# Bias products and turned row maxima on the full array, with zero rows, in a four-layer attention and expert kernel

## The reference

```
x += L0_xattn(layernorm(x), ctx)    # 16 heads of 8; biases on q, k, v and on the output
x += L0_ffn(layernorm(x))           # 8 experts, top 1, 128 -> 512 -> 128, gelu, biases b1, b2
x += L1_xattn(layernorm(x), ctx)    # 16 heads of 64, output bias
x += L1_ffn(layernorm(x))           # 128 -> 512 -> 128, rounded, piecewise linear gelu, biases
x += L2_xattn(layernorm(x), ctx)    # layernorm; self attention (causal) + ffn; layernorm; cross attention + ffn
x += L2_ffn(layernorm(x))           # 8 experts, top 2, silu, biases
x += L3_xattn(layernorm(x), ctx)    # 16 heads of 8, no bias
x += L3_ffn(layernorm(x))           # 8 experts, top 1, no bias on the output
```

## Time and profile before

| what | value |
|---|---|
| three runs | 1269.59, 1274.54 and 1707.18 us, median 1274.54 |
| span of the profiled execution | 1272.0 us |
| PE busy | 978.4 us (77%), 15468 products |
| DVE busy | 832.6 us (65%) |
| ACT busy | 735.7 us (58%) |
| POOL busy | 550.4 us (43%) |
| chain that ended last | PE 43%, DVE 25%, ACT 13%, issue 9%, POOL 5%, DMA 3% |
| mean granted TensorE clock | 0.870 of full speed |

### The profile page before, as it was taken

How to read it: one execution, slowest core, us unless ns; L and a number is a source line. 1 busy time by engine, 2 the same in 40 slices (tenths; PEclk the granted TensorE clock), 3 DMA queues, 4 the chain that set the end, 5 groups by cost and what they waited for, 6 DMA issues and landing times.

```text
span 1272.0 us, 38517 instructions
## 1 busy us (share of the span) xinstructions
PE 978.4 (77%) x15468; PEld 717.5 (56%) x15468; DVE 832.6 (65%) x2267; ACT 735.7 (58%) x1500; POOL 550.4 (43%) x575
## 2 busy tenths in 40 slices
PE   2778767989999867588998589988399956875874
PEld 1455556736767734345675256766287834654863
DVE  4667645688888588678877577767454647675532
ACT  5776454676665575576657467576265575763321
POOL 2565724345446344354361322221632475566132
PEclk9788678989999977799999699999599977786787
DMA  3321132211001010110001000000331121110122
GB/s 103 92 82 43 59 85 72 66 37 34 27 19 36 2 40 19 38 39 12 3 4 43 1 3 4 5 3 2 93 95 44 50 73 45 34 43 29 46 78 75
DMA packets 59727, 53.29 MB, mean 42 GB/s; under 512 B 10592, under 2 KB 47968, under 8 KB 59362
## 3 DMA queue, kind: packets, MB, share of 16 engines
q1 hardware_dynamic: 53777, 41.62, 11.4%
q0 software_dynamic: 4096, 8.40, 2.3%
q10 hardware_dynamic: 1683, 0.81, 0.2%
HBM read 33.90 MB, written 16.25 MB: 39 GB/s over the span
## 4 chain that ended last, share of the span: by engine, by line
PE 43%; DVE 25%; ACT 13%; issue 9%; POOL 5%; DMA 3%; POOLq 1%; ACTq 0%; SPq 0%; DVEq 0%
PE psum L698 16%; PE psum L1246 6%; PE psum L1264 5%; DVE area L1949 4%; POOL sorted_in L2882 3%; PE psum L821 2%; DVE stats L1930 2%; DVE negm L2085 2%; ACT area L1333 2%; ACT xn L1357 1%; PE psum L705 1%; DVE area L2117 1%; DVE x L2481 1%; PE psum L894 1%; PE psum L1223 1%
## 5 line engine op out<-in xcount | busy, mean ns | idle before, releaser
L1333 ACT ACTIVATE area<-psum 128x512 bf16<-128x512 f32 (+4 forms) x214 | 107.1, 525 | 126.0 <-PE psum L698 64.6
L1949 DVE TENSOR_TENSOR area<-psum,area 128x512 bf16<-128x512 f32 (+4 forms) x206 | 117.2, 601 | 44.3 <-ACT area L1333 43.2
L2592 DVE TENSOR_TENSOR area<-area 128x512 bf16<-128x512 f32 x106 | 73.1, 691 | 97.1 <-ACT area L1847 68.7
L1246 PE MATMUL psum<-xT_hi,moe 128*128 128x128 bf16 x848 | 111.0, 230 | 9.0 <-DVE xT_lo L1949 4.9
L2692 POOL TENSOR_TENSOR moe<-stage,moe 128x512 bf16<-128x512 f32 x47 | 54.8, 1168 | 123.2 <-ACT moe L1328 123.0
L1515 ACT ACTIVATE area<-psum 77x1024 f32<-77x1024 f32 (+1 forms) x96 | 92.8, 1017 | 23.8 <-PE psum L821 23.8
L1264 PE MATMUL psum<-moe,area 128*128 x1272 | 104.9, 224 | 0.9 <-DVE area L2601 0.9
L2085 DVE TENSOR_REDUCE negm<-psum 128x4 bf16<-128x308 f32 (+1 forms) x192 | 95.5, 540 | 12.4 <-PE psum L791 12.2
L1246 PEld LDWEIGHTS psum<-xT_hi,moe 128*128 x848 | 82.2, 103 | 20.8 <-issue 10.9
L1246 PE MATMUL psum<-xT_lo,moe 128*128 128x128 bf16 x424 | 93.7, 230 | 0.0
L1264 PEld LDWEIGHTS psum<-moe,area 128*128 128x128 bf16 x1272 | 85.3, 100 | 11.8 <-issue 1.4
(11 more groups left out here) (262 smaller groups left out, 2935.8 us busy)
## 6 DMA issues: line engine op xcount, KB each, us to landing
area<-sorted_in SPq DMA_DIRECT2D x22, 256.0 KB, 3.5
sorted_out<-area SPq DMA_DIRECT2D x22, 256.0 KB, 2.3
stage<-in_w_L0m SPq DMA_DIRECT2D x16, 256.0 KB, 2.9
stage<-in_w_L2m SPq DMA_DIRECT2D x16, 256.0 KB, 2.8
stage<-in_w_L3m SPq DMA_DIRECT2D x16, 256.0 KB, 2.7
sorted_in<-area SPq DMA_DIRECT2D x2, 1472.0 KB, 7.3
stage<-in_w_L2a SPq DMA_DIRECT2D x8, 320.0 KB, 3.3
stage<-in_w_L1x SPq DMA_DIRECT2D x6, 320.0 KB, 3.1
```

Of the source, the lines that this page charges most:

```text
L1246: ins = pe.matmul(bank[:, S * c:S * c + S], lhsT, v, start=n == 0, stop=n == 2)
L1333: ins = act.activation(out, bank, ACT.Copy)
L1949: ins = dve.tensor_tensor(out, bank, high, ALU.subtract)
L2592: dve.tensor_tensor(R.HL[u], R.HF[u], upper(R.HF[u]), ALU.subtract).then_inc(K.tile_split, tiles.one())
```

## The change

The tiles `pairs`, `pairs_L0b2`, `pairs_L2be2` and `ones` get 128 rows. POOL sets the three pair tiles to zero at the start, and DVE then writes the bias into rows 0 and 1 as before, so that a bias product uses 128 rows, 126 of them zero times one. In L1x the maxima go to a block of 128 x 128 (`A.NM`, two of them, in a tile that L1x does not use), which POOL sets to zero at the start of L1x; quarter `k` gets only its own four heads, at columns 36k to 36k+3, and one product turns the whole block. L2a1 and L2a2 keep the four products of 32 columns.

```diff
-        self.pairs = sb("pairs", [2, N_SHARED_PAIRS], BF16)
-        self.expert_pairs = {name: sb("pairs_" + name, [2, E * D], BF16) for name in ("L0b2", "L2be2")}
+        self.pairs = sb("pairs", [128, N_SHARED_PAIRS], BF16)
+        self.expert_pairs = {name: sb("pairs_" + name, [128, E * D], BF16) for name in ("L0b2", "L2be2")}
...
-        self.ones = sb("ones", [2, BANK], BF16)
+        self.ones = sb("ones", [128, BANK], BF16)
...
+        self.NM = [K.yT_hi[:, s, 0:128] for s in range(2)]
...
-            for r in range(4):
-                ins = pe.matmul(bank[32 * r:32 * r + 32, 0:S], K.negm[:, b % 2, :], K.ident_bf[:, :], start=True, stop=True)
+            if A.upright:
+                for r in range(4):
+                    ins = pe.matmul(bank[32 * r:32 * r + 32, 0:S], K.negm[:, b % 2, :], K.ident_bf[:, :], start=True,
+                                    stop=True)
+            else:
+                ins = pe.matmul(bank[:, 0:S], A.NM[b % 2], K.ident_bf[:, :], start=True, stop=True)
             filled(ins, name, "negm", b)
...
         sem.wait_ge(K.pair_copied, 1)
+        sem.wait_ge(K.pairs_zeroed, 1)
         for out, (at, n) in [(K.pairs, (0, N_SHARED_PAIRS))] + [(v, PAIRS[name]) for name, v in K.expert_pairs.items()]:
-            dve.scalar_tensor_tensor(out[:, :], K.pair_hi[:, at:at + n], K.col("pmask")[0:2, :],
+            dve.scalar_tensor_tensor(out[0:2, :], K.pair_hi[:, at:at + n], K.col("pmask")[0:2, :],
                                      K.pairs_raw[:, at:at + n], ALU.mult, ALU.add)
...
-                empty(dve.tensor_reduce(K.negm[:, s, 4 * k:4 * k + 4],
+                if A.upright:
+                    out = K.negm[:, s, 4 * k:4 * k + 4]
+                else:
+                    sem.wait_ge(K.negm_zeroed, 1)
+                    out = A.NM[s][:, 36 * k:36 * k + 4]
+                empty(dve.tensor_reduce(out,
...
     def start():
+        for v in [K.pairs] + list(K.expert_pairs.values()):
+            ins = pool.memset(v[:, :].bitcast(F32), 0.0)
+        ins.then_inc(K.pairs_zeroed, 1)
         pool.memset(K.ones[:, :], 1.0)
...
+        if not A.upright:
+            for v in A.NM:
+                ins = pool.memset(v.bitcast(F32), 0.0)
+            ins.then_inc(K.negm_zeroed, 1)
```

More of the change, by code:

```diff
@@ L199, in __init__ @@
         self.pair_hi = self.carve(AREA - D - (N_FIRST_PAIRS + 1) // 2, (N_FIRST_PAIRS + 1) // 2, BF16)[0:2, 0:N_FIRST_PAIRS]
-        self.late_raw, self.late_pairs = self.expert_pairs["L0b2"][:, :].bitcast(F32), self.expert_pairs["L0b2"][:, 0:F]
+        self.late_raw, self.late_pairs = self.expert_pairs["L0b2"][0:2, :].bitcast(F32), self.expert_pairs["L0b2"][:, 0:F]
         self.late_hi = self.routing.rearrange("p b n -> p (b n)")[0:2, 128:128 + F // 2].bitcast(BF16)
@@ L252, in __init__ @@
         self.head_rows_set, self.values_preset = sem("head_rows_set"), sem("values_preset")
+        self.negm_zeroed = sem("negm_zeroed")
         self.maxima_zeroed, self.values_zeroed = sem("maxima_zeroed"), sem("values_zeroed")
@@ L261, in __init__ @@
         self.steps_ready = sem("steps_ready")
+        self.pairs_zeroed = sem("pairs_zeroed")
         self.zero_set, self.sort_ready, self.every_set = sem("zero_set"), sem("sort_ready"), sem("every_set")
@@ L2184, in attention @@
                 sem.wait_ge(K.pair_copied, 2)
-                dve.scalar_tensor_tensor(K.late_pairs, K.late_hi, K.col("pmask")[0:2, :], K.late_raw, ALU.mult, ALU.add)
+                dve.scalar_tensor_tensor(K.late_pairs[0:2], K.late_hi, K.col("pmask")[0:2, :], K.late_raw, ALU.mult, ALU.add)
             if b == B - 3:
```

## The result

| what | before | after |
|---|---|---|
| median of 12 executions each, in turn on one chip | 1272.41 us | 1261.68 us |
| span of the profiled execution | 1272.0 us | 1261.6 us |
| mean granted TensorE clock | 0.870 | 0.875 |

The ratio is 0.9924 with an interval of [0.9906, 0.9942], so the kernel became 7 to 12 us faster. The forecast was 1258 us, 14 us less than before; the likeliest case came about, with a gain some 4 us smaller. Single executions that a disturbance lengthened (here one of the kernel before, 1707.18 us) are in no ratio of this document, and the profile of e8, which is of such an execution, is not read.

A forecast was written before the change was run, and what follows sets the result against it. PE was taken to set the end where its shape changes stand in the chain of waits. 4.5 + 5.3 + 2.4 + 0.8 + 1.7 - 0.6 = 14.1 us off 1272.0 us gave 1258 us, range 1243 to 1273 us.

The forecast's parts named there:

- the likeliest case: Whole kernel: the forecast itself, 1258 us, with its own bounds 1249 to 1265 us; chance 0.68.
- The drain: On PE: the extra 0.09 to 0.10 us whenever a product's rows or columns in use differ from its neighbour's.
- L1x, 4.5 us: L1x: full bias and one turning product save 3.7 us in 12 steps and 0.8 us in four.
- Feed-forward, 5.3 + 2.4 us: Full biases save 28 x 0.19 = 5.3 us in L2f1 and L2f2, and 2.4 us in L1f.
- a rival that falls in a whole long stage: L1x: the granted clock falls to L1f's, costing 22 us, so the kernel takes 1280 us; chance 0.07.
- Experts, 1.7 us: L0m and L2m: sequencer hides most of the cost; 0.03 us for 58 tiles, ends 0 and 11.0 us.
- the pair of rows: Profile rows: an L2m tile with bias takes 1.17 us, an L3m tile without bias 1.16 us.
- the first rival: Expert stages: the sequencer does not hide the cost; 9.3 us more there, 1246 us in all; chance 0.13.
- The sign that was named for the first rival: L2m: a tile 0.15 us shorter in the changed profile would mean that the sequencer does not hide the cost.
- L2a1 and L2a2, -0.6 us: Row maxima wait for the full bias: a loss of 0.8 us, less two gains of 0.1 us each.
- L0x, 0.8 us, and the memsets, 0: L0x: four biases save 0.19 us each; three memsets at the start and two in L1x cost nothing.
- The sum: Whole kernel: all terms together save 14.1 us of the profiled execution's 1272.0 us, giving 1258 us.

The follow-up runs named there:

- e8: Changed kernel with the experts' bias added twice at full rows, against the kernel before: 1302.70 us against 1311.87 us, ratio 0.9928.
- e2: Kernel before with only L1x's maxima turned by one product, every bias at 2 rows: 1310.77 us against 1311.76 us, ratio 0.9999.
- e6: Changed kernel with L1x's maxima turned by four products again, all biases full, against the kernel before: 1298.19 us against 1311.87 us, ratio 0.9893.
- e9: Kernel before with only L1x changed, full output bias and one turning product: 1271.73 us against 1269.82 us, ratio 1.0008.
- e11: The kernel before again, nothing changed, one profiled execution: 1265.68 us, where that chip's median for the kernel before is 1269.82 us.
- e10: Kernel before with only the biases of the expert stages at full rows: 1273.54 us against 1269.82 us, ratio 1.0023.
- e1: The changed kernel as it stands, again, against the kernel before on the same chip: 1296.92 us against 1311.76 us, ratio 0.9898.
- e4: Changed kernel with the experts' biases back at 2 rows, against the kernel before: 1300.78 us against 1311.76 us, ratio 0.9921.
- e7: Changed kernel with the experts' bias added twice at 2 rows, against the kernel before: 1305.36 us against 1311.87 us, ratio 0.9945.
- e3: Changed kernel with the output biases of L2a1 and L2a2 back at 2 rows, against the kernel before: 1298.39 us against 1311.76 us, ratio 0.9900.
- e5: Kernel before with only the biases of L1f, L2f1 and L2f2 at full rows: 1307.41 us against 1311.87 us, ratio 0.9962.

## Why the prediction was right, step by step

*The drain, and that zero rows remove it.* Shown, as to the steps. In the twelve steps of L1x each of the three long ones became 0.056 us (0.31 to 0.216 us at 512 columns), and e2 and e6 show that a neighbour of another shape brings them back. Why such a step is longer is argued: the array may empty first, or the load for another shape may not be taken ahead. The extra 0.09 to 0.10 us is also as long as one load (0.10 us in the rows), and no run separates the two. The rule that was weighed against the sum (the Trainium skill, "TensorE: Matmul & The Clock Gate", Part 3, under what overlaps: a load overlaps only for another row group) does not hold here: full products with a load each of 0.10 us follow at 0.056 us, where a load that waited for its neighbour could not. The allowance in Part 2 of the same page of the Trainium skill, step by step, for loads into a background buffer agrees with these rows.

*L1x, 4.5 us.* Measured 6.2 us in two pairs and 4.5 us in e9. The step from 0.48 to 0.17 us is exact; the excess in the pairs comes with a clock that was at 1.2 GHz for 12.3 and 6.8 us of L1x before and 3.4 us twice after. Kernels with the same 6.8 us at 1.2 GHz in L1x, though on different chips, differ by the term: 193.0 and 192.7 us without the change (e11, e10), 188.9, 188.2 and 189.9 us with it (e1, e4, e7), that is 3.9 us.

*Feed-forward, 5.3 + 2.4 us.* L1f gave 3.9 us, 1.5 us more than its term, again with less time at 1.2 GHz (38.9 and 41.0 us before, 30.7 and 34.1 us after); e2 and e3, on one chip and with the same 37.5 us of it, are 2.9 us apart in L1f (75.9 and 73.0 us). L2f1 with L2f2 gave only 0.7 us of 5.3 (+1.0 and -1.7 us). Here is the term that was mis-sized: the drains went nearly as counted, 2.1 to 2.9 us in a stage at the same clock, and the stretches at 1.2 GHz took it back in L2f1 each time and in L2f2 in two of three executions. The prediction priced the clock only as a rival that falls in a whole long stage, and not as something that shifts by a few us between stages.

*Experts, 1.7 us.* Right in kind: the drains cost nothing there (e7 against e8, e10, and L2m at 112.8 and 112.6 us). But the pair of rows that it rested on was luck. It compared one tile of L2m (1.17 us) with one of L3m (1.16 us); over all such tiles of the kernel before the medians are 1.28 and 1.12 us, which would have read as 0.16 us a tile for the bias, near the first rival. The runs refute that reading; the pair of rows by itself could not. The size was too high; its lower bound, 0, is what the runs show. The sign that was named for the first rival, a tile shorter by 0.15 us, is not there.

*L2a1 and L2a2, -0.6 us.* The place looks as forecast, 0.20 us from the last full product to the row maxima. Its size lies under the noise of these stages, and e3 against e1 can't tell it.

*L0x, 0.8 us, and the memsets, 0.* L0x moved by -0.2 us, within its noise of 1.6 us between two executions of the same kernel. The three memsets at the start took 1.5 us together and the two in L1x 0.15 us each, and nothing in the profile waits for them: the stretch up to L0x is 19.2 and 19.3 us after, 19.7 and 19.2 us before.

*The sum.* That it came within 4 us is in part luck. By the table L1x and L1f gave 3.2 us more than their terms, L2f1 with L2f2 4.6 us less, and the other stages account for the rest.

*What stays open.* The parts alone sum to less than the whole: e5 -5.0, e9 +1.0 and e10 +2.9 us by their ratios, in sum -1.1 us (with L0x and L2a left out), against -9.7 us of the whole by the ratio of the result and -13.4 us by e1's, each single term with some 3.5 us of uncertainty. By the slope above the clock accounts for 3.8 + 2.0 = 5.8 us of the 9 to 12 us that are missing; the rest is about what such a sum of three can be off. That the clock is the whole reason is not shown, and what sets where it falls was not found.

## What to carry to other kernels

In this kernel a lone product with few rows among full ones cost about 0.19 us (0.15 us in and out, where a like neighbour costs 0.056 us), whatever its duration in the profile says: look at starts, not at durations, and pad it with zeros to its neighbours' shape. Where two such products stand side by side, pad both: either alone gives less than its half. Do it where PE sets the end and its products follow one another as fast as they can; beside the products at computed offsets of the expert stages it was worth nothing, and ahead of a product of yet another shape the drain only moves. A gain of under 1% can't be summed from parts tried alone: measure the whole, and read the granted clock of each stage beside its length.

## What the hardware showed that I had not expected

The same kernel took 1312 us on two chips and 1270 us on another, and the changed one 1297 and 1262 us. L2m is most of it: 137.7 us long in e1, 112.2 us in the profile after (stage lengths as in the table above). Groups of products by line, first of e1, then of the kernel after (busy us, mean ns | idle before, and what ended it):

```profile
L1254 PE MATMUL psum<-xT_hi,moe 128*128 128x128 bf16 x848 | 117.1, 237 | 23.1 <-issue 18.2 <-DVE xT_lo L1957 3.0 <-ACT area L1855 1.4
L1272 PE MATMUL psum<-moe,area 128*128 x1272 | 113.6, 228 | 22.4 <-issue 21.0 <-DVE area L2615 0.9
```

```profile
L1254 PE MATMUL psum<-xT_hi,moe 128*128 128x128 bf16 x848 | 112.3, 230 | 9.1 <-DVE xT_lo L1957 4.5 <-issue 3.5 <-ACT area L1855 0.6
L1272 PE MATMUL psum<-moe,area 128*128 x1272 | 107.7, 223 | 1.7 <-DVE area L2615 0.9
```

On that chip PE stands still in the middle of a tile, while the profile shows nothing it waits for; the timeline of e1 in L2m:

```profile
915.71 0.68 PE L1272 MATMUL psum<-moe,area 128*128 x5
916.89 0.28 PE L1272 MATMUL psum<-moe,area 128*128 x2 [0.51 <-issue]
918.31 0.28 PE L1272 MATMUL psum<-moe,area 128*128 x2 [1.14 <-issue]
919.72 0.37 PE L1272 MATMUL psum<-moe,area 128*128 x2 [1.14 <-issue]
```

Two products at a time, then 1.14 us of nothing. What it is was not tried. It is in L2m of all seven kernels that were read on those chips (134 to 140 us), with 2-row and full biases alike. It cancels in a comparison within a chip only as far as it repeats, so the lengths of the expert stages in e4 and e7 say nothing of a few us; e10 was timed on a chip that doesn't have it.
